# A routed LayerNorm moved ahead of a rotation, the first loads split over two queues, and one wait shortened in a gated cross-attention and expert kernel

## The chip, the cores and the metric

The kernel runs on one core of a Trainium2 chip. The metric is the device time of one execution in microseconds (us). The program is written engine by engine: TensorE (PE, with its weight loads as PEld), VectorE (DVE), ScalarE (ACT), GpSimd (POOL) and the DMA queue of SyncE (SP) each have an instruction stream of their own, and all order between them is by semaphores that the program counts by hand. An engine executes its stream in order, so an instruction that waits holds up everything behind it on that engine.

## The reference

The input x holds 16 batches of 112 rows of 512 values. Each batch has a context of 375 rows of 128 values.

```python
x = x + tanh(g_xattn[0]) * xattn(layernorm(x), ctx, ...)   # 16 heads, latent scores, rotation of q and of the context
x = x + tanh(g_ffn[0])   * ffn(layernorm(x), ...)          # 64 experts, 8 chosen for each row, and one shared expert
```

The attention projects the normalised x for each head (`Wq`), turns the result into a 384-wide latent (`w_kc_q`), rotates it with tables of cosines and sines, folds it with `W_qr` and `W_kr` into 128 values that meet the rotated context, and takes a softmax. The feed-forward part sends each row of the second normalised x to the 8 experts with the highest logits.

## The kernel before

The 16 batches are worked in four groups of four (`GB`). A group has two stages.

**The head stage** is a loop over h from 0 to 17 in `tensor`, `vector`, `scalar`, `gpsimd` and `sync` alike. In its turn h, TensorE projects head h (`project`, 12 products of 448 columns), makes the latent of head h-1 (`latent`, 9 products, lines 822 to 824 in both cases), and takes head h-2 to the context space (`to_context`, line 926). DVE makes the low half of each projection (line 1245), multiplies the latent with the cosine and sine tables in seven operations a head (`latent`, lines 1270 and 1274), and makes the low half of what goes to the context space (line 1280). GpSimd adds the cosine and sine parts in three operations a head (line 1940). ACT makes the high halves.

**The score stage** is a loop over 56 tiles of scores (`RT` = 14 for each batch) with softmax, transposes (line 955) and the product with the context. The output projection of the group follows (`out_head`), and DVE adds it to x (line 1342).

**The routing** of finished batches is woven into the head stage of the next group. `slots(g, i)` gives each step of batch i of group g a slot, `between(g, slot)` lists the steps of a slot, and turn h of the head loop carries slots 2h and 2h+1. For the first batch of a group the steps are statistics in slot 0 (DVE line 1323, then GpSimd lines 1904 and 1906 with the power of -0.5), "norm" in slot 2 (DVE line 1399), "turn" in slot 3 (TensorE's four transposes, line 1028, and ACT's copy, line 1741), "router" in slot 4 (line 1040), "choose" in slot 5. On DVE, slot 2 stands behind the seven operations of head 0's rotation; slots 0 and 1 stand ahead of the projection of head 1. On TensorE and ACT nothing stands between slot 2 and slot 3 of turn 1. SP stores the normalised rows and the new x (`finish` in `sync`, lines 666 and 667) `STORE_LAG` = 4 slots after their "norm", so for the first batch at the head of turn 3, behind its reloads of weights.

**The end of the last group.** Batches 13 to 15 have nothing to hide their routing behind. When the last tiles of scores are under way, TensorE begins the output projection of batch 15 (`out_head` with p = `NG`); it goes into bank 7, which also holds the ranks of batch 12. Ahead of its first head TensorE waits until all of batch 12's routing steps are counted:

```python
if p == NG and h == 0:
    pe.wait_ge(s_exp, RT * B)
    pe.wait_ge(s_route, NR * (B - GB + 1))
```

DVE reads the ranks in the first operation of `put_in_place` (line 1376); three more operations make the places and one adds to the count (line 1384). GpSimd's scatters of batches 13, 14 and 15 (line 1962) come after that, and the experts after them.

**The start.** SP issues the identity matrix and the constant -0.5 (lines 538 and 539, both on semaphore `s_first`), then the four batches of x (line 544), then weights. DVE waits for `s_first`, writes five small pads, takes statistics of the four batches, and normalises batches 0 and 1 into two buffers (`xn1`). Batches 2 and 3 are normalised in the same two buffers once TensorE has transposed the batch before (`s_xt`), between the low halves (line 1234) of batches 0 and 1. ACT copies the first weights (line 1667) ahead of the high halves of x (line 1646). TensorE's first projection needs all four batches.

Of the kernel before, what the change touches and what calls it, by code (L numbers as in the profile page):

```python
# [11 lines left out]
ALU = mybir.AluOpType  # L12
# [4 lines left out]
B, S, C = 16, 112, 512  # L17
# [5 lines left out]
P = 128  # L23
# [6 lines left out]
GB = 4  # L30
# [30 lines left out]
def shape_constants():  # L61

    sq, cq = rope_tables(S, Q)
    sk, ck = rope_tables(L, D)

    sr = np.concatenate([-sq[:, :QH], sq[:, QH:]], axis=1)
    skn = np.concatenate([-sk[:, :D // 2], sk[:, D // 2:]], axis=1)
    cq, sr = cq[:, PERM], sr[:, PERM]
    sr[:, 2 * QW:] = np.concatenate([sr[:, -QW // 2:], sr[:, 2 * QW:-QW // 2]], axis=1)
    qt = lambda a: np.ascontiguousarray(a.T.reshape(QC, QW, S).transpose(1, 0, 2))  # L70
    lt = lambda a: np.ascontiguousarray(a.reshape(LJ, LP, D).transpose(1, 0, 2))
    tri = np.triu(np.ones((S, S), np.float32), 1)
    return {
        "c_cos_q": qt(cq), "c_sin_q": qt(sr), "c_cos_k": lt(ck), "c_sin_k": lt(skn),
        "c_ident": np.eye(P, dtype=np.float32),
        "c_before": tri,
        "c_ones": np.ones((S, P), np.float32),
        "c_expert": np.tile(np.arange(E, dtype=np.float32), (S, 1)),
        "c_minus_half": np.full((P, 1), -0.5, np.float32),


        "c_spare": np.ascontiguousarray(np.arange(P * (3 * NY + 1), dtype=np.float32).reshape(3 * NY + 1, P).T),
        "c_own_row": SPARE + np.arange(S, dtype=np.float32)[:, None] * KY + np.arange(TOP, dtype=np.float32),
        "c_expert_entries": np.tile(np.arange(E, dtype=np.float32) * SPAN, (S, 1)),
        "c_lower_first": np.tile(-np.arange(E, dtype=np.float32) / E, (E, 1)),
        "c_lower_own": -np.arange(E, dtype=np.float32)[:, None] / E,
        "c_number": np.tile(np.arange(E, dtype=np.float32)[:, None], (1, P)),
        "c_caps": np.asarray(CAPS, np.float32)[None, :],
    }
# [46 lines left out]
def slots(g, i):  # L136

    at = START[LEFT[g]][i]
    whole = {"turn": at + 3, "router": at + 4, "choose": at + 5, "rank": at + 7, "place": at + 8}
    if g:  # L140
        whole.update({f"scatter {k}": at + 9 + (k * 7 // 8 if i == 2 else k) for k in range(TOP)})
    return {"stats": max(0, at - 2), "norm": max(2, at), **(whole if i < GB - LEFT[g] else {})}

# [98 lines left out]
def x_bank(b):  # L242
    return 4 + b if b < GB else 7
# [39 lines left out]
def build(nc, a, out):  # L283
    with ExitStack() as ctx:
# [3 lines left out]
        def sem(name):  # L288
            return ctx.enter_context(nc.semaphore(name))
# [108 lines left out]
        q_t = [sb(f"q_t{p}", [D, GB, H, S], F32R) for p in "hl"]  # L398

        def q_rows(part, b, at, width):  # L400
            return q_t[part][:, b % GB, :, :].rearrange("d h s -> d (h s)")[:, at:at + width]
# [44 lines left out]

        s_first, s_const, s_late, s_zero = sem("s_first"), sem("s_const"), sem("s_late"), sem("s_zero")
        s_const_k = sem("s_const_k")
# [88 lines left out]
        def sync(sp):  # L537
            sp.dma_start(ident[:], a["c_ident"]).then_inc(s_first, 16)
            sp.dma_start(minus_half[:], a["c_minus_half"]).then_inc(s_first, 16)

            def load_x(b):
# [126 lines left out]

            for b in range(GB):
                load_x(b)  # L670
            load_wq(0)
# [147 lines left out]
        def tensor(pe):  # L819
# [6 lines left out]
            def turn_x(b):  # L826
# [7 lines left out]
                for j in range(CJ):  # L834
                    m = pe.transpose(bank[x_bank(b)][:, j * S:(j + 1) * S], xn1[b % 2][:, j * P:(j + 1) * P],
                                     ident[0:S, 0:S])
# [140 lines left out]
            def out_head(p, h, part):  # L977
# [13 lines left out]
                if p == NG and h == 0:  # L991
                    pe.wait_ge(s_exp, RT * B)
                    pe.wait_ge(s_route, NR * (B - GB + 1))
                if part != "first":
# [61 lines left out]

            pe.wait_ge(s_first, 32)
            for b in range(GB):
# [155 lines left out]
        def vector(dve):  # L1214
# [9 lines left out]
            def norm_x(b):  # L1224
                st = ln_stats[min(b, GB)]
                if b >= 2:
                    dve.wait_ge(s_xt, b - 1)
                dve.wait_ge(s_rs1, 2 * (b + 1))
                dve.tensor_scalar(xn1[b % 2][:], x_sb[b % NX][:], st[:, 6:7], st[:, 0:1], ALU.subtract, ALU.mult)\
                   .then_inc(s_nm1, 1)  # L1230
# [187 lines left out]

            dve.wait_ge(s_first, 32)
            for part in (*kv_t[0], *kv_t[1]):  # L1420
                dve.tensor_scalar(part[:, L:L + 1], ident[:, 0:1], 0.0, None, ALU.mult).then_inc(s_pad, 1)
            dve.memset(count[:], 0.0).then_inc(s_pad, 1)
            for b in range(GB):
                stats_x(b)
            norm_x(0)
            norm_x(1)
            for b in range(GB):
                turn_x(b)
                if b + 2 < GB:
                    norm_x(b + 2)  # L1430

# [209 lines left out]
        def scalar(act):  # L1641
# [94 lines left out]
            def finish(step, b):  # L1736
# [6 lines left out]
                if step == "choose":  # L1743
                    act.wait_ge(s_route, NR * b + R_SHIFT)
                    act.activation(raised[:], top[:], ACT.Exp, bias=small[:, 0:1], accum_out=small[:, 1:2])\
                       .then_inc(s_weigh, 1)

            split_wq(0)
            for b in range(GB):
# [151 lines left out]
        def gpsimd(pool):  # L1901
# [62 lines left out]

            pool.wait_ge(s_first, 32)
            for b in range(GB):
# [123 lines left out]
```

## Time and profile before

| | |
|---|---|
| median of 3 runs | 1543.54 us (1543.45 to 1543.58) |
| the profiled execution, own time | 1545.0 us |
| its span in the profile | 1543.1 us |
| PE busy | 1419.2 us, 92% |
| DVE busy | 1147.3 us, 74% |
| POOL busy | 783.3 us, 51% |
| ACT busy | 672.1 us, 44% |

The span is the time between the first and the last instruction that the profile shows; 1.9 us of the execution lie around it. Busy times of different engines overlap. A matmul's duration is modelled and reaches over the start of the next one, so the step from start to start is its cost in a chain. The rows quoted further down give the start in us, the duration in us, the engine, the line, the operation with output and input, and in brackets how long the engine had been idle before and what ended the idleness.

### The profile page before, as it was taken

To read this page: it belongs to the slowest core of one execution; us is meant where nothing else is said; L and a number is where in the kernel's file an instruction comes from. 1 tells how busy PE (TensorE), PEld (TensorE's weight loads), DVE (VectorE), ACT (ScalarE), POOL (GpSimd) and SP (SyncE) were. 2 spreads that over 40 slices of the span, in tenths; PEclk is the share of its full clock that TensorE was granted. 3 is DMA by queue.
4 is the path that set the end of the run, shared out by engine and by line. 5 is a ranking of instruction groups with operands and counts; after the bars stand their busy time and mean duration, and the time that the engine had idled before them with its cause. 6 is when DMAs were issued, how large, how long until landed. Compare 5 with 4: busy or idle time off the path is not lost.

```text
span 1543.1 us, 25067 instructions
## 1 busy us (share of the span) xinstructions
PE 1419.2 (92%) x7674; PEld 1165.1 (76%) x7674; DVE 1147.3 (74%) x2601; ACT 672.1 (44%) x1558; POOL 783.3 (51%) x858
## 2 busy tenths in 40 slices
PE   6999899899999989999989999986399999989985
PEld 5767787777788777778877778864388999979742
DVE  5777783298987269989528988544488999979587
ACT  3332673011476011177301137431277777867521
POOL 4555673145775458877345786325344344334322
PEclk9999999999999999999999999998599999999998
DMA  7898896355697757830365763295899999999698
GB/s 238 298 313 314 274 286 193 112 167 188 215 307 219 265 162 246 253 122 8 104 217 191 243 216 113 86 341 180 239 331 327 332 357 366 373 339 338 206 429 344
DMA packets 164359, 380.10 MB, mean 246 GB/s; under 512 B 20200, under 2 KB 55682, under 8 KB 162434
## 3 DMA queue, kind: packets, MB, share of 16 engines
q1 hardware_dynamic: 136182, 286.33, 55.5%
q0 software_dynamic: 20608, 62.28, 11.8%
q10 hardware_dynamic: 7436, 29.88, 6.0%
q8 instruction: 64, 1.05, 0.3%
q14 instruction: 69, 0.57, 0.1%
HBM read 238.82 MB, written 139.59 MB: 245 GB/s over the span
## 4 chain that ended last, share of the span: by engine, by line
PE 71%; DVE 10%; DMA 9%; issue 5%; POOL 2%; ACT 2%; SPq 1%; POOLq 0%; another core or an unknown queue 0%; DVEq 0%; ACTq 0%
PE bank L822 18%; PE bank L824 17%; PE bank L823 17%; PE bank L926 8%; PE bank L955 4%; DMA p_in<-parts 3%; PE bank L1124 2%; DMA parts<-y_sb,to_row 1%; DMA w_ex<-in_w_ex 1%; PE bank L914 1%; PE bank L904 1%; DMA out<-p_sum 1%; DVE prob_t0l L1309 1%; POOL slot_rows L1962 1%; ACT prob L1705 1%
## 5 line engine op out<-in xcount | busy, mean ns | idle before, releaser
L1940 POOL TENSOR_TENSOR q_rope<-q_rope,q_sin 128x448 f32<-128x448 f32 x192 | 215.7, 1153 | 147.4 <-DVE q_sin L1274 146.8
L2020 POOL DMA_INDIRECT parts<-y_sb,to_row x140 | 138.3, 988 | 221.0 <-ACT y_sb L1846 191.4
L1946 POOL TENSOR_TENSOR prob<-prob,row_inv 128x375 f32<-128x375 f32 x219 | 176.8, 814 | 88.7 <-DVE row_inv L1296 86.5
L1962 POOL DMA_INDIRECT slot_rows<-rows,pos_i x112 | 109.7, 980 | 104.2 <-DVE count L1384 76.8
L1274 DVE TENSOR_TENSOR q_sin<-bank,sin_q 128x448 f32<-128x448 f32 (+1 forms) x256 | 158.5, 619 | 4.0
L926 PE MATMUL bank<-q_rope,m_w 128*128 128x448 f32 x384 | 155.7, 541 | 2.8 <-issue 1.8
L1288 DVE TENSOR_REDUCE row_max<-bank 128x1 f32<-128x375 f32 x224 | 118.9, 535 | 36.8 <-PE bank L824 36.4
L1705 ACT ACTIVATE prob<-bank,row_max 128x375 f32<-128x375 f32 x224 | 128.3, 573 | 9.1 <-DVE row_max L1288 9.1
L1846 ACT ACTIVATE y_sb<-bank,own 96x512 f32<-96x512 f32 (+4 forms) x140 | 90.9, 687 | 68.6 <-PE bank L824 62.0
L955 PE MATMUL bank<-ident,prob 128*125 128x128 f32 x672 | 113.6, 279 | 7.1 <-DVE prob_t0l L1309 3.6
L1270 DVE TENSOR_TENSOR q_rope<-bank,cos_q 128x448 f32<-128x448 f32 x192 | 118.3, 616 | 0.0
L955 PEld LDWEIGHTS bank<-ident,prob 128*125 128x125 f32 x672 | 103.6, 189 | 15.9 <-POOL prob L1946 13.1
L926 PEld LDWEIGHTS bank<-q_rope,m_w 128*128 128x128 f32 x384 | 71.5, 189 | 53.4 <-issue 50.3
L1688 ACT ACTIVATE q_th<-bank 128x448 fp32r<-128x448 f32 x64 | 34.9, 545 | 170.6 <-PE bank L926 156.4
L1681 ACT ACTIVATE q_hk0h<-bank 128x448 fp32r<-128x448 f32 x32 | 17.5, 546 | 160.4 <-PE bank L824 160.4
L1720 ACT ACTIVATE prob_t0h<-bank 125x384 fp32r<-125x384 f32 x128 | 63.0, 492 | 46.0 <-PE bank L955 46.0
L1124 PE MATMUL bank<-ident,x_g 96*128 96x96 f32 (+4 forms) x560 | 64.5, 261 | 20.0 <-DMA x_g<-slot_rows 20.0
L1124 PEld LDWEIGHTS bank<-ident,x_g 96*128 96x128 f32 (+4 forms) x560 | 59.5, 144 | 29.6 <-DMA x_g<-slot_rows 20.5
L822 PE MATMUL bank<-xg_t0h,w_gu_s0h 128*128 128x224 f32 (+5 forms) x256 | 75.9, 297 | 4.9 <-DVE e_half L1529 4.9
L1342 DVE SCALAR_TENSOR_TENSOR x_sb<-bank,tanh_g,x_sb 112x512 f32<-112x512 f32 x16 | 11.3, 746 | 88.5 <-PE bank L824 88.5
L822 PE MATMUL bank<-xg_t1h,w_gu_s1h 128*128 128x224 f32 (+5 forms) x256 | 73.9, 289 | 0.7 <-DVE e_half L1529 0.6
L823 PE MATMUL bank<-xg_t0l,w_gu_s0h 128*128 128x224 f32 (+5 forms) x256 | 73.2, 286 | 0.0
(364 smaller groups left out, 4399.1 us busy)
## 6 DMA issues: line engine op xcount, KB each, us to landing
w_ex<-in_w_ex SPq DMA_DIRECT2D x64, 768.0 KB
slot_rows<-blank SPq DMA_DIRECT2D x64, 612.0 KB
p_in<-parts SPq DMA_DIRECT2D x14, 2048.0 KB, 16.9
m_w<-m_dram SPq DMA_DIRECT2D x48, 192.0 KB
x_g<-slot_rows ACTq DMA_DIRECT2D x16, 476.0 KB
wq_s0h<-wq_dram SPq DMA_DIRECT2D x24, 256.0 KB
wq_s0l<-wq_dram SPq DMA_DIRECT2D x24, 256.0 KB
wq_s1h<-wq_dram SPq DMA_DIRECT2D x24, 256.0 KB
```

The lines of the kernel that those rows point to most:

```text
L822: pe.matmul(out_ap, wh, mh, start=first, stop=False)
L823: pe.matmul(out_ap, wh, ml, start=False, stop=False)
L824: return pe.matmul(out_ap, wl, mh, start=False, stop=last)
L926: m = pe.matmul(bank[5][:, 0:GT], m_w[n % NW][:, c, :], q_rope[h % 2][:, c, :], start=(c == 0), stop=(c == QC - 1))
L955: m = pe.transpose(bank[bk][0:LP, j * P:(j + 1) * P], prob[n % NP][:, j * LP:(j + 1) * LP], ident[:])
L1124: m = pe.transpose(bank[n % 3][:, j * size:(j + 1) * size], x_g[x % NXE][0:size, t, j * P:(j + 1) * P], ident[0:size, 0:size])
L1274: dve.tensor_tensor(q_sin[to:to + size, other, :].rearrange("p (b s) -> p b s", b=GB), src[at:at + size], table, ALU.mult).then_inc(s_rope, 1)
L1705: act.activation(prob[i][:], bank[score_bank(n)][:, 0:L], ACT.Exp, bias=row_max[:, i:i + 1], accum_out=row_sum[:, i:i + 1]).then_inc(s_exp, 1)
L1940: pool.tensor_tensor(o[:, c, :], o[:, c, :], q_sin[:, c, :], ALU.add).then_inc(s_radd, 1)
L1946: pool.tensor_tensor(prob[i][:], prob[i][:], row_inv[:, i:i + 1].to_broadcast([P, L]), ALU.mult)\
L1962: pool.indirect_dma_start(slot_rows, bass.IndirectOffsetOnAxis(ap=pos_i[i][:, k:k + 1], axis=0), rows[i][:], None).then_inc(s_slots[i], 16)
L2020: pool.indirect_dma_start(parts, bass.IndirectOffsetOnAxis(ap=to_row[x % NROW][0:size, t:t + 1], axis=0), y_sb[x % NY][t][0:size, :], None)\
```

## The change

For the first batch of each group's routing, "norm" goes to slot 1 and "turn" to slot 2. The loads of x alternate between SP (batches 0 and 2) and ACT (batches 1 and 3), and the identity follows them. The constant -0.5 is written by GpSimd instead of loaded. The normalised batches 2 and 3 of the first group go into two of the `rows` buffers, which are free at the start, so that all four are normalised in a row, ahead of the low halves and the pads. The wait ahead of batch 15's output projection asks for batch 12's ranks to be read (`R_RANKED`), not for its count.

```diff
-        "c_minus_half": np.full((P, 1), -0.5, np.float32),
...
-    whole = {"turn": at + 3, "router": at + 4, "choose": at + 5, "rank": at + 7, "place": at + 8}
+    whole = {"turn": at + (3 if i else 2), "router": at + 4, "choose": at + 5, "rank": at + 7, "place": at + 8}
...
-    return {"stats": max(0, at - 2), "norm": max(2, at), **(whole if i < GB - LEFT[g] else {})}
+    return {"stats": max(0, at - 2), "norm": at if i else 1, **(whole if i < GB - LEFT[g] else {})}
...
+        def xn1_of(b):
+            return rows[b - 2][:, 0:C] if 2 <= b < GB else xn1[b % 2][:]
...
         def sync(sp):
-            sp.dma_start(ident[:], a["c_ident"]).then_inc(s_first, 16)
-            sp.dma_start(minus_half[:], a["c_minus_half"]).then_inc(s_first, 16)
-
...
-            for b in range(GB):
-                load_x(b)
+            load_x(0)
+            load_x(2)
+            sp.dma_start(ident[:], a["c_ident"]).then_inc(s_first, 16)
             load_wq(0)
...
                 if p == NG and h == 0:
                     pe.wait_ge(s_exp, RT * B)
-                    pe.wait_ge(s_route, NR * (B - GB + 1))
+                    pe.wait_ge(s_route, NR * (B - GB) + R_RANKED)
...
-            pe.wait_ge(s_first, 32)
+            pe.wait_ge(s_first, 16)
...
             def norm_x(b):
                 st = ln_stats[min(b, GB)]
-                if b >= 2:
+                if b >= GB:
                     dve.wait_ge(s_xt, b - 1)
...
-            dve.wait_ge(s_first, 32)
+            for b in range(GB):
+                stats_x(b)
+            for b in range(GB):
+                norm_x(b)
+            for b in range(GB):
+                turn_x(b)
+            dve.wait_ge(s_first, 16)
             for part in (*kv_t[0], *kv_t[1]):
                 dve.tensor_scalar(part[:, L:L + 1], ident[:, 0:1], 0.0, None, ALU.mult).then_inc(s_pad, 1)
             dve.memset(count[:], 0.0).then_inc(s_pad, 1)
-            for b in range(GB):
-                stats_x(b)
-            norm_x(0)
-            norm_x(1)
-            for b in range(GB):
-                turn_x(b)
-                if b + 2 < GB:
-                    norm_x(b + 2)
...
+            for b in (1, 3):
+                act.dma_start(x_sb[b][:], a["x"][b * S:(b + 1) * S, :]).then_inc(s_x[b], 16)
             split_wq(0)
...
-            pool.wait_ge(s_first, 32)
+            pool.memset(minus_half[:], -0.5).then_inc(s_half, 1)
+            pool.wait_ge(s_half, 1)
             for b in range(GB):
                 spread(ln_stats[b], s_bn1, s_rs1, b)
```

## Rows read from the trace of the kernel before

**Rows 1.** The page: the chain that ended last, shares of the span by engine.

```profile
PE 71%; DVE 10%; DMA 9%; issue 5%; POOL 2%; ACT 2%; SPq 1%; POOLq 0%; another core or an unknown queue 0%; DVEq 0%; ACTq 0%
```

**Rows 2.** PE's waits: instruction, releaser: us in total, times, longest.

```profile
PE bank L1028 <- DVE rows L1399: 19.3, 4, 7.9
...
PE bank L1028 <- DVE early_rows L1399: 4.2, 1, 4.2
```

**Rows 3.** Timeline of PE at the start of the second group's head stage.

```profile
292.62 0.36 PE L822 MATMUL bank<-xn_th,wq_s0h 128*128 128x448 f32 x1
...
297.49 0.37 PE L822 MATMUL bank<-q_hk0h,wcq_s0h 128*128 128x448 f32 x1
...
303.65 1.01 PE L1028 MATMUL bank<-ident,early_rows 112*128 112x112 f32 x4 [4.17 <-DVE early_rows L1399]
...
309.95 0.91 PE L1040 MATMUL bank<-token_w,xn_t 128*112 128x64 f32 x8
```

**Rows 4.** Timeline of PE: the same two steps in the third and fourth groups.

```profile
554.35 1.01 PE L1028 MATMUL bank<-ident,rows 112*128 112x112 f32 x4 [4.17 <-DVE rows L1399]
561.47 0.91 PE L1040 MATMUL bank<-token_w,xn_t 128*112 128x64 f32 x8
...
806.42 1.01 PE L1028 MATMUL bank<-ident,rows 112*128 112x112 f32 x4 [4.17 <-DVE rows L1399]
813.78 0.91 PE L1040 MATMUL bank<-token_w,xn_t 128*112 128x64 f32 x8
```

**Rows 5.** Stretches: start:end, length, busy of PE, PEld, DVE, ACT, POOL, PEclk, DMA, GB/s.

```profile
304.00:307.00 3.00, 3.00 (x11) 2.74 (x10) 0.00 (x0) 0.54 (x1) 0.59 (x1) 0.50 0.03 10
...
330.00:340.00 10.00, 10.00 (x40) 7.35 (x39) 9.84 (x20) 1.29 (x3) 4.49 (x6) 1.00 0.48 156
```

**Rows 6.** Timeline of PE: the same transposes at full clock.

```profile
502.79 0.55 PE L1028 MATMUL bank<-ident,rows 112*128 112x112 f32 x4
```

**Rows 7.** Timelines of POOL and DVE around the second group's first norm.

```profile
297.67 0.57 POOL L1906 TENSOR_TENSOR ln_stats<-ln_stats,minus_half 112x1 f32<-112x1 f32 x1
301.09 3.50 POOL L1940 TENSOR_TENSOR q_rope<-q_rope,q_sin 128x448 f32<-128x448 f32 x3 [2.86 <-DVE q_sin L1274]
...
298.26 0.62 DVE L1245 TENSOR_TENSOR q_hk1l<-bank,q_hk1h 128x448 fp32r<-128x448 f32 x1 [0.99 <-ACT q_hk1h L1681]
...
302.89 0.71 DVE L1399 TENSOR_SCALAR early_rows<-x_sb,ln_stats 112x512 f32<-112x512 f32 x1
```

**Rows 8.** Timelines around the wait ahead of batch 15's output projection (DVE, PE, POOL).

```profile
1041.49 0.20 DVE L1376 TENSOR_TENSOR rank_sb<-bank,expert_entries 112x64 f32<-112x64 f32 x1
...
1043.98 0.55 DVE L1309 TENSOR_TENSOR prob_t0l<-bank,prob_t0h 125x384 fp32r<-125x384 f32 x1
...
1044.32 0.74 PE L822 MATMUL bank<-v_w0h,q_th 128*112 128x512 f32 x1 [3.23 <-DVE count L1384]
...
1064.53 0.94 POOL L1962 DMA_INDIRECT slot_rows<-rows,pos_i  x1 [10.51 <-DVE count L1384]
```

**Rows 9.** Stretch from that matmul on; columns as in rows 5.

```profile
1044.30:1048.20 3.90, 3.88 (x13) 3.18 (x14) 0.23 (x1) 0.33 (x1) 2.99 (x4) 0.56 0.48 91
```

**Rows 10.** Timelines of the first 16 us: SP's issues of x, then DVE, ACT, PE.

```profile
1.65 1.83 SPq L544 DMA_DIRECT2D x_sb<-in_x  x4
...
8.20 0.69 DVE L1220 BATCH_NORM_STATS2 ln_stats<-x_sb 112x6 f32<-112x512 f32 x1
...
0.74 1.28 ACT L1667 ACT_TABLE_LOAD   x1 [0.74 <-PEq L2081]
9.27 0.64 ACT L1667 ACTIVATE wq_s0h<-wq 128x512 fp32r<-128x512 f32 x1 [7.25 <-DMA wq<-in_w_q]
...
9.69 1.73 PE L835 MATMUL bank<-ident,xn 112*128 112x112 f32 x8 [9.69 <-DVE xn L1229]
12.41 2.00 PE L835 MATMUL bank<-ident,xn 112*128 112x112 f32 x8 [1.00 <-DVE xn L1229]
15.79 0.71 PE L822 MATMUL bank<-xn_th,wq_s0h 128*128 128x448 f32 x1 [1.38 <-DVE xn_tl L1234]
```

More of the change, by code:

```diff
@@ L445, in build @@
         base_in = early_base + [x for _, x in late_tiles]
-        s_first, s_const, s_late, s_zero = sem("s_first"), sem("s_const"), sem("s_late"), sem("s_zero")
+        s_half, s_first, s_const, s_late, s_zero = sem("s_half"), sem("s_first"), sem("s_const"), sem("s_late"), sem("s_zero")
         s_const_k = sem("s_const_k")
@@ L834, in turn_x @@
                 for j in range(CJ):
-                    m = pe.transpose(bank[x_bank(b)][:, j * S:(j + 1) * S], xn1[b % 2][:, j * P:(j + 1) * P],
+                    m = pe.transpose(bank[x_bank(b)][:, j * S:(j + 1) * S], xn1_of(b)[:, j * P:(j + 1) * P],
                                      ident[0:S, 0:S])
@@ L1225, in norm_x @@
                 st = ln_stats[min(b, GB)]
-                if b >= 2:
+                if b >= GB:
                     dve.wait_ge(s_xt, b - 1)
                 dve.wait_ge(s_rs1, 2 * (b + 1))
-                dve.tensor_scalar(xn1[b % 2][:], x_sb[b % NX][:], st[:, 6:7], st[:, 0:1], ALU.subtract, ALU.mult)\
+                dve.tensor_scalar(xn1_of(b), x_sb[b % NX][:], st[:, 6:7], st[:, 0:1], ALU.subtract, ALU.mult)\
                    .then_inc(s_nm1, 1)
```

## The prediction

> **What bounds the kernel now.** I read the chain that ended last, then PE's waits, then the timelines at the places where PE waited. TensorE holds 71% of the chain [rows 1], so time is gained only where PE stands idle or runs slowly. PE's waits name the transposes of the routed rows among the largest items, with VectorE's norm as the releaser: four times in `rows` and once in `early_rows` [rows 2]. The timeline puts three of them at the same place of the second, third and fourth group, each after exactly 4.17 us of idle time [rows 3, 4]. There PE has finished head 0's latent and comes to "turn", while the norm is still behind head 0's rotation on DVE: DVE begins it at 302.89, although GpSimd had its scale ready at 297.67 + 0.57 = 298.24 [rows 7]. After each idle stretch PE works at half clock, 0.50 for the 3 us from 304 to 307 [rows 5]. The largest remaining `rows` wait, 7.9 us, belongs to batch 15 at the end, which the change does not touch.
>
> **Norm and turn.** "Norm" passes from slot 2 to slot 1: on DVE it moves ahead of head 1's low half and head 0's seven rotation operations. "Turn" passes from slot 3 to 2, with nothing between them on PE and ACT, so their orders stay. What matters is whether the rows are ready when PE arrives. In the first head stage 24 products run from 292.62 to 297.49, 0.203 us a step, and nine more bring PE to the transposes at 299.32 [rows 3]. The norm can start at 298.24 and takes 0.71 [rows 7], so it ends at 298.95, 0.37 ahead. I take the wait as gone.
>
> The price of a group goes from idle start to the router. Now: 4.17 idle and 309.95 - 303.65 = 6.30 of work [rows 3], 7.12 and 7.36 in the next two groups [rows 4]. The work is four transposes, 12 products and 9 products. At full clock the transposes take 0.55 [rows 6] and 21 products 21 x 0.203 = 4.26, in all 4.81. The groups give back 4.17 + 1.49, 4.17 + 2.31 and 4.17 + 2.55, together **18.9 us**. If the clock fell all the same, 12.5 would be left; nothing that PE would wait for here makes it fall. The upper end is 19.6, since the last transpose's 0.2 overlaps the next product.
>
> What becomes late next: DVE's low half of head 1 starts at 298.95 instead of 298.26, and so the rotation of head 0 and GpSimd's three adds come 0.7 later, the adds at 301.8 to 305.3 instead of 301.09 to 304.59 [rows 7]. PE needs the first of them at 299.32 + 4.81 + the router's 0.91 = 305.0, and the last only after two thirds of that step. So that costs nothing, but the cover shrinks to some tenths of a us; without it the 0.7 would be paid three times, 2.1. From then on DVE has little air: it is busy 9.84 of 10 us in a later stretch of the stage, with PE busy throughout [rows 5]. It starts at most 0.7 later in relation to PE than before, and each head's output goes through double buffers, so I put this at nothing, with the 2.1 in the range. On GpSimd, the scatters of slots 0 and 1 stand ahead of the adds in the third and fourth group, as now; they had time while DVE worked, and their order does not change. SP stores the rows and the new x one place earlier, ahead of the next reload of projection weights and behind one reload of `m_w`; two issues of 0.46 (a quarter of 1.83, [rows 10]) delay that reload by 0.9, and it is needed a whole head later. Nothing, and at worst 0.9 for each group.
>
> **Batch 15's projection.** PE stands idle for 3.23 us until 1044.32 for batch 12's count, while the ranks had been read at 1041.49 + 0.20 = 1041.69 [rows 8]. With the shorter wait PE goes on some 0.1 later, 2.5 us sooner. What follows is the next-to-last tile, then the last tile, which cannot start before DVE's split that begins at 1043.98 and ends at 1044.53 [rows 8]; so a short idle returns there. Against this stands the clock: 3.90 us at 0.56 after the old wait [rows 9] cost some 3.90 x 0.44 = 1.7, of which part comes back if it stays up. Lower end 1.5 (the split is waited for and the clock falls again), upper end 3.5, taken **2.5**. It reaches the end: GpSimd's scatters of batch 13 had been idle for 10.51 us until 1064.53 [rows 8], and they and all behind them follow from this PE work.
>
> **The start.** The last batch of x is issued last of four on SP, at 1.65 + 1.83 = 3.48, its statistics begin at 8.20, and PE's first product at 15.79 [rows 10]. That is 7.59 from statistics to product. With four buffers the transposes of four batches follow each other: the first starts 9.69 - 8.20 = 1.49 after the last statistics, two batches take 1.73, the other two 2.00, then a high and a low half of some 0.55 and 0.62 and a few tenths of handing over, about 6.5. That is 1.05 without any earlier transfer. ACT's two issues can be out by 1.7 if they go ahead of the table load, or by 2.94 if they stand behind its end at 2.02 [rows 10]: 1.8 or 0.5 earlier than 3.48. The weights' copy on ACT at 9.27 [rows 10] stands ahead of the high halves; its load is issued 1.4 earlier, and if it landed at 9.27 as now, the high halves would still be done before the transposes allowed more. Pads on DVE, GpSimd's memset in place of a load and the later identity are all ready before anything needs them, which costs nothing; if the five pads stood in the way, 0.4. Together 1.05 + 0.5 to 1.05 + 1.8, with 4.5 as the far end if the half-speed stretch after the first product moved too; taken **2.5**.
>
> The long time from issue to statistics, 8.20 - 3.48 = 4.72 for one batch, looks like transfers that share what moves them. The Trainium skill ("DMA: Bandwidth & Descriptors", "Issuing engines are not separate DMA queues") says that loads started by different engines run on the same 16 DMA engines, and that issuing from several saves only sequencer time. By that the second queue brings no bandwidth, and the start's term would be the first rival's below; no row before shows two queues loading x at once, so the trace leaves it open.
>
> **Sum.** 18.9 + 2.5 + 2.5 = 23.9 us. Against the profiled execution, 1545.0 - 23.9 = 1521.1. That execution lies 1.5 above the median of 1543.54, so the median should come to 1519.6; I say 1519.5.
>
> **The rivals.**
>
> Start without a gain from transfers: x lands when it does now, because the DMA engines are the limit. Then the start gives 1.05, and the median is 1543.5 - 18.9 - 2.5 - 1.05 = 1521.0. For it speaks that PE's start hangs on 4.7 us of transfer; against it, that the first issue is 0.9 earlier. Chance 0.2.
>
> Only the idle time returns: the clock falls at other places instead, or the 0.37 us margin of the norm is not there and PE still stops briefly. Then three times 4.17, 1.5 and 1.05 are left, 15.1, which gives 1528.4. For it speaks the small margin and the shrunken cover on GpSimd; against it that all PE waits of this stage disappear with the norm. Chance 0.14.
>
> Slower: DVE executes in order, and in slot 1 it waits for GpSimd's power with head 1's low half and the whole rotation behind it, which before had nothing to wait for. If GpSimd is late by d, PE loses d less about 1 us in each group, and the half clock besides. The point from which this is slower than now is d = 23.9 / 3 + 1 = 9 us a group; with d = 12 the time would be 1543.5 + 9 = 1552.5. It needs GpSimd to be held up by scatters ahead of the statistics. In the group shown it had answered by 298.24 [rows 7], so there is no such d. Chance 0.02.
>
> The change does not do what it says, because the turn on PE is held by something else that came at the same time as the norm: no gain but the start and the end, 1538.5, chance 0.02. No gain at all, chance 0.02.
>
> **How the numbers follow.** The forecast as summed has 0.6. The range takes the start's far end, the clock's return and the rest of a late 0.7 us, and reaches most of the way to the second rival: 1515.5 to 1527.0. A measurement of this kernel tells about 0.2%, 3.1 us, from no change. Forecast and first two rivals are all well over that and so is most of the fourth: faster 0.95; "no gain" and a part of the fourth make same 0.03; slower 0.02.
>
> **What would show it.** In the new profile, the three 4.17 us gaps ahead of the routed transposes should be gone, the granted clock should stay at 1.00 there, and transposes to router should take 4.8. DVE's norm should stand ahead of head 1's low half. The wait for the count should be a wait for the ranks of under 1 us, with a new short wait ahead of the last tile's transposes. The first product should start near 13.3. I would be wrong if a new wait for GpSimd's adds or for reloaded weights stood in the second to fourth head, or if PE lost elsewhere what it gained at the turns.

## The result, and the profile after

The changed kernel takes 1522.31 us (median of 4 runs, 1521.71 to 1524.49), the kernel before 1543.56 in the same comparison. The ratio is 0.9864, with a 95% interval of 0.9847 to 0.9881: 18 to 24 us faster. The forecast was 1519.5 with a range of 1515.5 to 1527.0. The profiled execution of after took 1521.71 us of its own time, with a span of 1519.9; that of before had a span of 1543.1, so the two profiles differ by 23.2.

Below, "lead" is how much earlier than in the profile of before an instruction of TensorE starts. Line numbers of the new kernel are 2 to 4 lower: the routed transposes are L1026, the norm L1397, the router L1038, the products L820 to L822.

First the busy times of the page of after.

```profile
PE 1407.8 (93%) x7674; PEld 1156.0 (76%) x7674; DVE 1148.8 (76%) x2601; ACT 672.3 (44%) x1558; POOL 783.2 (52%) x859
```

PE is busy 11.4 us less than the 1419.2 of before with the same instructions. The work behind the three turns, which no longer runs at the lower clock, makes 6.7 of that by the rows below. PE still holds 70% of the chain that ended last [rows 1]. The rest of the gain is idle time.

PE's waits (instruction, releaser: us in total, times, longest) answer to [rows 2].

```profile
PE bank L1026 <- DVE rows L1397: 10.9, 2, 7.8
...
PE bank L953 <- POOL prob L1944: 3.7, 1, 3.7
...
PE bank L820 <- DMA wq_s1l<-wq_dram: 1.2, 1, 1.2
...
PE bank L820 <- DMA wq_s0l<-wq_dram: 1.0, 1, 1.0
```

The wait for `early_rows` is gone and that for `rows` has two cases in place of four. The 7.8 us case is batch 15's at the end, as before. Two short waits for reloaded weights stand out, 1.2 and 1.0; in the profile of before they were 0.4 and 0.2.

The timeline of PE at the three places of [rows 3, 4], in the second, third and fourth group:

```profile
298.66 0.55 PE L1026 MATMUL bank<-ident,early_rows 112*128 112x112 f32 x4
...
303.38 0.91 PE L1038 MATMUL bank<-token_w,xn_t 128*112 128x64 f32 x8
...
543.43 0.55 PE L1026 MATMUL bank<-ident,rows 112*128 112x112 f32 x4
...
548.10 0.91 PE L1038 MATMUL bank<-token_w,xn_t 128*112 128x64 f32 x8
...
789.39 0.55 PE L1026 MATMUL bank<-ident,rows 112*128 112x112 f32 x4
...
794.05 0.91 PE L1038 MATMUL bank<-token_w,xn_t 128*112 128x64 f32 x8
```

No idle time stands in brackets, and the transposes take 0.55 in place of 1.01. From transposes to router it is 4.72, 4.67 and 4.66 us, where it was 6.30, 7.12 and 7.36. A stretch of that work (start:end, length, busy of PE, PEld, DVE, ACT, POOL, granted clock, DMA, GB/s) answers to the 0.50 of [rows 5]:

```profile
299.00:302.00 3.00, 3.00 (x18) 2.74 (x16) 2.97 (x6) 0.81 (x2) 1.10 (x1) 1.00 0.58 152
```

On DVE and GpSimd the same place now reads as follows (compare [rows 7]).

```profile
297.01 0.57 POOL L1904 TENSOR_TENSOR ln_stats<-ln_stats,minus_half 112x1 f32<-112x1 f32 x1
300.90 3.36 POOL L1938 TENSOR_TENSOR q_rope<-q_rope,q_sin 128x448 f32<-128x448 f32 x3 [3.32 <-DVE q_sin L1272]
...
297.62 0.55 DVE L1397 TENSOR_SCALAR early_rows<-x_sb,ln_stats 112x512 f32<-112x512 f32 x1 [1.00 <-POOL ln_stats L1904]
298.08 0.62 DVE L1243 TENSOR_TENSOR q_hk1l<-bank,q_hk1h 128x448 fp32r<-128x448 f32 x1
```

The norm stands ahead of head 1's low half and ends at 298.17, some 0.5 us ahead of PE's 298.66. The bracket on the norm is the one new wait in this stage, and it costs nothing: before, DVE stood the same time there, 0.99 us, for ACT's high half [rows 7].

The start, in the timelines of SP's and ACT's queues, DVE and PE, answers to [rows 10]:

```profile
0.73 0.87 SPq L541 DMA_DIRECT2D x_sb<-in_x  x2
0.73 0.91 ACTq L1745 DMA_DIRECT2D x_sb<-in_x  x2
...
6.52 0.66 DVE L1218 BATCH_NORM_STATS2 ln_stats<-x_sb 112x6 f32<-112x512 f32 x1
...
7.97 1.73 PE L833 MATMUL bank<-ident,xn 112*128 112x112 f32 x8 [7.97 <-DVE xn L1227]
8.20 2.48 DVE L1227 TENSOR_SCALAR rows<-x_sb,ln_stats 112x512 f32<-112x512 f32 x2
10.28 1.75 PE L833 MATMUL bank<-ident,rows 112*128 112x112 f32 x8 [0.58 <-DVE rows L1227]
13.42 0.71 PE L820 MATMUL bank<-xn_th,wq_s0h 128*128 128x448 f32 x1 [1.39 <-DVE xn_tl L1232]
```

The first product starts at 13.42, 2.37 earlier. The last issue of x ends at 1.64 in place of 3.48, and its statistics begin at 6.52 in place of 8.20.

At the end (compare [rows 8]):

```profile
1022.10 0.20 DVE L1374 TENSOR_TENSOR rank_sb<-bank,expert_entries 112x64 f32<-112x64 f32 x1
...
1022.56 0.46 PE L820 MATMUL bank<-v_w0h,q_th 128*112 128x512 f32 x1 [0.86 <-DVE rank_sb L1374]
...
1025.28 0.56 PE L953 MATMUL bank<-ident,prob 128*125 128x128 f32 x3 [0.78 <-DVE prob_t0l L1307]
...
1038.22 0.94 POOL L1960 DMA_INDIRECT slot_rows<-rows,pos_i  x1 [3.60 <-DVE count L1382]
```

The wait is for the ranks, 0.86 long, and a new one of 0.78 stands ahead of the last tile's transposes.

Following the lead through the kernel tells where the time came from and where some went. It is 2.4 at the first product, but only 0.7 at 172 us, in group 0's score stage. It rises by 5.9, 6.8 and 7.0 at the three turns, stands at 19.4 before batch 15's projection and at 26.3 after it, and is 23.2 at the end.

The loss at 172 us has this view, of SP's queue, GpSimd, PE and two stretches, and no row in the prediction:

```profile
157.55 0.35 SPq L643 DMA_DIRECT2D kv_raw<-in_ctx  x1
...
163.72 0.99 POOL L1921 TENSOR_TENSOR kv_full<-kv_raw,cos_k 125x384 f32<-125x384 f32 x1 [3.91 <-DMA kv_raw<-in_ctx]
...
165.53 1.00 PE L953 MATMUL bank<-ident,prob 128*125 128x128 f32 x3 [3.69 <-POOL prob L1944]
...
162.50:167.50 5.00, 1.97 (x8) 1.97 (x9) 1.39 (x4) 0.93 (x3) 3.78 (x6) 0.72 1.05 376
167.50:172.50 5.00, 5.00 (x19) 4.18 (x19) 1.63 (x6) 2.21 (x7) 4.09 (x5) 0.60 0.97 309
```

The same place in the profile of before:

```profile
160.05 0.36 SPq L646 DMA_DIRECT2D kv_raw<-in_ctx  x1
...
165.61 0.99 POOL L1923 TENSOR_TENSOR kv_full<-kv_raw,cos_k 125x384 f32<-125x384 f32 x1 [3.29 <-DMA kv_raw<-in_ctx]
...
167.42 1.00 PE L955 MATMUL bank<-ident,prob 128*125 128x128 f32 x3 [3.10 <-POOL prob L1946]
```

GpSimd waits 3.91 us for the context of the second batch, with its scaling of probabilities behind it, and PE waits 3.69 for these; before, the waits were 3.29 and 3.10. The load is issued 2.50 earlier than before, as much as PE is ahead there, so this transfer moved along with the rest; in this execution it took 0.6 longer. The larger part, 1.2 us, goes behind the wait: over the 5 us from the end of the wait the granted clock is 0.50, and over the same 5 us in the profile of before it is 0.69. The earlier start is neither needed for this loss nor enough for it. The kernel with the shorter wait only, whose start is that of before, takes 1.1 us more than before behind the same wait, at a clock of 0.50. The changed kernel's second profile takes 0.1 more at the wait and 0.1 more behind it, at a clock of 0.67. How long the lower clock lasts behind this wait comes and goes with the execution.

### The profile page after: what moved, and what is told of

It is laid out like the page before. It is cut to its first block, busy times and chain, and to the rows that moved or that the text cites. A ratio compares the mean times of both kernels' runs of the same rounds, so it can differ in the third digit from the quotient of the medians.

```text
span 1519.9 us, 25065 instructions
## 1 busy us (share of the span) xinstructions
PE 1407.8 (93%) x7674; PEld 1156.0 (76%) x7674; DVE 1148.8 (76%) x2601; ACT 672.3 (44%) x1558; POOL 783.2 (52%) x859
## 3 DMA queue, kind: packets, MB, share of 16 engines
q0 software_dynamic: 20608, 62.28, 12.1%
q8 instruction: 64, 1.05, 0.3%
## 4 chain that ended last, share of the span: by engine, by line
PE 70%; DMA 12%; DVE 9%; issue 4%; POOL 3%; ACT 2%; SPq 0%; POOLq 0%; ACTq 0%; DVEq 0%
PE bank L820 18%; PE bank L822 17%; PE bank L821 17%; PE bank L924 9%; PE bank L953 4%; DMA p_in<-parts 3%; DMA w_ex<-in_w_ex 3%; DMA parts<-y_sb,to_row 3%; PE bank L1122 2%; POOL slot_rows L1960 1%; PE bank L912 1%; PE bank L1038 1%; PE bank L902 1%; DVE prob_t0l L1307 1%; DMA out<-p_sum 1%
## 5 line engine op out<-in xcount | busy, mean ns | idle before, releaser
L820 PE MATMUL bank<-xg_t0h,w_gu_s0h 128*128 128x224 f32 (+5 forms) x256 | 74.8, 292 | 4.2 <-DVE e_half L1525 4.2
L820 PE MATMUL bank<-xg_t1h,w_gu_s1h 128*128 128x224 f32 (+5 forms) x256 | 73.8, 288 | 5.1 <-DVE e_half L1525 5.0
```

The lines of the kernel that those rows point to most:

```text
L820: pe.matmul(out_ap, wh, mh, start=first, stop=False)
```

## The experiments

Eleven kernels ran, in three sets. Kernels of a set share a chip and its runs of the kernel before. Its median was 1543.68 in the first set, 1547.01 in the second and 1547.79 in the third. Single runs of one kernel lie several us apart, so I read ratios with their intervals and, for what is smaller, places in the traces. A ratio is an estimate from all the runs and not the quotient of the two medians.

### First set: each part of the change alone

**Slots only.** The kernel before with

```diff
-    whole = {"turn": at + 3, "router": at + 4, "choose": at + 5, "rank": at + 7, "place": at + 8}
+    whole = {"turn": at + (3 if i else 2), "router": at + 4, "choose": at + 5, "rank": at + 7, "place": at + 8}
...
-    return {"stats": max(0, at - 2), "norm": max(2, at), **(whole if i < GB - LEFT[g] else {})}
+    return {"stats": max(0, at - 2), "norm": at if i else 1, **(whole if i < GB - LEFT[g] else {})}
```

> Only norm and turn one slot earlier. Theory A (the turn waits and their slow stretches are the main gain, parts add up): all three 4.17 us gaps gone, 19 to 20 us less than before. Rival B (what is gained at the turns is partly lost again to late weight loads, because the stores of the first batch now stand ahead of a reload): one or two new DMA waits of about 1 us ahead of a projection, directly behind the moved stores (fourth head of a group), and only 17 to 18 us less.

Measured: 1524.14 (5 runs), ratio 0.9868 (0.9845 to 0.9890), 19.5 us by the medians. This part alone is most of the change. The one wait for a reloaded weight that stands out is 0.6 us long. Of its two edits only the one of "norm" does anything: with "turn" put back to `at + 3` in the changed kernel, the instructions stand in the same order on all five engines, since slots 2 and 3 belong to the same turn of the loop. That is read from the order of the programs and needed no run.

**Start only.** The kernel before with the loads over two queues and the four buffers, and with what goes along with them: the identity behind x, the -0.5 written by GpSimd, the pads behind the norms. The diff shows the main lines.

```diff
-            for b in range(GB):
-                load_x(b)
+            load_x(0)
+            load_x(2)
+            sp.dma_start(ident[:], a["c_ident"]).then_inc(s_first, 16)
...
+            for b in (1, 3):
+                act.dma_start(x_sb[b][:], a["x"][b * S:(b + 1) * S, :]).then_inc(s_x[b], 16)
...
-                dve.tensor_scalar(xn1[b % 2][:], x_sb[b % NX][:], st[:, 6:7], st[:, 0:1], ALU.subtract, ALU.mult)\
+                dve.tensor_scalar(xn1_of(b), x_sb[b % NX][:], st[:, 6:7], st[:, 0:1], ALU.subtract, ALU.mult)\
```

> Only the start. Theory A (everything behind the start shifts with it): first product near 13.4 us instead of 15.8, time 2.4 us less. Rival B (the context of batch 1 lands when the DMA lets it, so the score stage of the first group eats the lead): first product near 13.4 too, but the lead of 2.4 falls to 0.6 to 1.9 at 165 us, with a longer PE wait for GpSimd's normalised tile (3.7 us instead of 3.1), time 0.5 to 2 us less.

**Loads only.** The same without the four buffers (norms and turns interleaved over two buffers, as before).

> The loads over two queues, the later identity, GpSimd's -0.5 and the pads behind, but two buffers as before. Theory A (both halves of the start's change count: earlier landing 1.3, four buffers 1.05): first product near 14.5 us. Rival B (the transfers land when the DMA engines allow, so only issue time is saved): first product 15.3 or later. Time between 0.3 and 1.5 us less than before.

Measured: start 1542.39, ratio 0.9979 (0.9960 to 0.9998); loads alone 1543.90, ratio 0.9987 (0.9972 to 1.0001). The first interval ends just short of 1 and the second includes it, so only the traces tell the parts. PE's first product, in the kernel with loads only and in that with both:

```profile
7.75 1.73 PE L832 MATMUL bank<-ident,xn 112*128 112x112 f32 x8 [7.75 <-DVE xn L1226]
...
13.86 0.71 PE L819 MATMUL bank<-xn_th,wq_s0h 128*128 128x448 f32 x1 [1.39 <-DVE xn_tl L1231]
```

```profile
7.94 1.73 PE L835 MATMUL bank<-ident,xn 112*128 112x112 f32 x8 [7.94 <-DVE xn L1229]
...
13.39 0.71 PE L822 MATMUL bank<-xn_th,wq_s0h 128*128 128x448 f32 x1 [1.39 <-DVE xn_tl L1234]
```

The loads bring the first product from 15.79 to 13.86, 1.93. From the first transposes to it the two-buffer kernel needs 6.11 us (6.10 before), the four-buffer one 5.45: the buffers give 0.65, not 1.05. These are single profiles: in the other kernels with the new start the first product comes at 13.23 to 13.47 six times, and at 14.37 and 14.94 where x landed later; in those with the old one at 15.15, 15.71 and 15.79. At 172 us the lead of the kernel with both has fallen from 2.4 to 1.2. That is the number of the expectation's rival, but not its mechanism: PE's wait for the context is 3.0 us, not 3.7, and the time goes behind it, at the lower clock.

**The shorter wait only.**

```diff
-                    pe.wait_ge(s_route, NR * (B - GB + 1))
+                    pe.wait_ge(s_route, NR * (B - GB) + R_RANKED)
```

> Only the wait ahead of batch 15's output projection. Theory A (as predicted: the idle time and a part of the clock): 2.5 us less than before, at most 3.5. Rival B (the short gap also keeps the clock at 1.00 through the heads behind it, and takes the later wait for the turned rows along): 6 to 7 us less, GpSimd's scatter of batch 13 starts 6 to 7 us earlier.

Measured: 1540.74, ratio 0.9981 (0.9967 to 0.9996), 0.6 to 5.1 us. The lead grows by 6.9 us at this place in the profile of after, and by 6.2 here, against 2.5 forecast. The three kernels of this set that keep the long wait show why that comparison misleads. From the transposes ahead of the wait to those of the routed rows behind it (1040.53 to 1052.58 in the profile of before) they take 12.47, 12.50 and 12.54 us, before 12.05; with the shorter wait it is 9.78 here and 9.11 after. That is 2.3 to 3.4, about 3. The lower figure is the one at which the clock fell again: behind the short wait it is 0.57 for 4.0 us here, and 1.00 in the profile of after. The rest of the lead, some 3.5 us, belongs to the profile of before alone; the kernel with the start only gains as much there with the long wait. In its timeline PE goes on at 1056.22 after a wait for `xn_t`; the kernel with the start only, same code at this place, has none:

```profile
1052.58 0.55 PE L1028 MATMUL bank<-ident,rows 112*128 112x112 f32 x4
...
1055.53 0.54 ACT L1741 ACTIVATE xn_t<-bank 128x448 f32<-128x448 f32 x1 [1.06 <-remote]
...
1056.22 0.97 PE L1040 MATMUL bank<-token_w,xn_t 128*112 128x64 f32 x8 [2.40 <-ACT xn_t L1741]
```

```profile
1052.46 0.55 PE L1028 MATMUL bank<-ident,rows 112*128 112x112 f32 x4
...
1053.04 0.55 ACT L1739 ACTIVATE xn_t<-bank 128x448 f32<-128x448 f32 x1
...
1053.73 0.97 PE L1040 MATMUL bank<-token_w,xn_t 128*112 128x64 f32 x8
```

From one to the other it is 3.64 us in the first and 1.27 in the second. What held ACT, the trace does not name.

### Second set: variants of the changed kernel

> The changed kernel once more, as the measure for its variants and for the spread. Theory: the comparison of the profile of before with those of three kernels that keep its routed batch as it is shows that the profile of before holds two stretches of its own: a 2.4 us wait for xn_t at 1056 and half clock from 1058 to 1061, which the others lack (they gain 2.7 to 3.0 us between 1031 and 1060 against it), and an experts stage of 433.6 us from the second wait for x_g to the end, where the others take 435.5 to 436.7. If so, this execution again has neither the xn_t wait nor an experts stage under 435, and its median is 1519 to 1524. Rival: the expert stage of the changed kernel is longer because of the change; then a stage of 436 here as well, but kernels with the slots as before would not have shown it.

Measured: 1521.80, ratio 0.9853 (0.9825 to 0.9880). The expectation held for the time and for the experts stage: 436.2 us, counted from the second wait for gathered rows, where the profile of before has 433.6 and the twelve others of this study 433.4 once and 434.4 to 436.7 eleven times. So the 2.5 us that the change seemed to hand back there need no cause in it: the three other kernels with the old slots show 435.4 to 436.7 against this one execution of before. It failed for the late `xn_t`: transposes to router took 2.36 us, where the first profile of this same kernel has 1.27. So the delay is not made by the change. The four kernels of the first set all have 1.27 or 1.28, the seven of the other two sets all 2.29 to 3.35, the profile of before 3.64; it goes with the set of runs, and its cause is open.

**The second batch's context earlier.** In SP's program:

```diff
+                    if g == 0 and h == 12:
+                        load_context(1)
...
-                        if t == 0 and g == 0:
-                            load_context(1)
```

> The changed kernel with the load of the second batch's context issued in the thirteenth head of group 0 instead of behind the last weight store. Theory: group 0's score stage hands back part of the earlier start because GpSimd stands 3.9 us for this load, and PE 3.7 us for GpSimd's prob, after which it works at 0.60 to 0.72 for 10 us. Then this wait is gone, PE's lead at the end of the stage grows by 3.7 to 6.5 us, and the median is 4 to 6 us under that of the changed kernel. Rival: another wait stands right behind it (the copy of x ahead of the score stage, ACT or DVE), and 1 to 2 us come out. Second rival: the load is not what is late (the wait named is an inference), nothing changes.

Measured: 1518.58 (5 runs, 1514.84 to 1520.64), ratio 0.9811 (0.9789 to 0.9832). The changed kernel has 0.9853 in the same set. The timeline and stretches of this kernel:

```profile
125.08 0.35 SPq L643 DMA_DIRECT2D kv_raw<-in_ctx  x1
...
161.27 1.01 POOL L1921 TENSOR_TENSOR kv_full<-kv_raw,cos_k 125x384 f32<-125x384 f32 x1
...
163.69 0.56 PE L953 MATMUL bank<-ident,prob 128*125 128x128 f32 x3
...
160.00:165.00 5.00, 4.27 (x26) 3.55 (x26) 5.00 (x13) 4.30 (x14) 4.07 (x6) 1.00 0.91 294
165.00:170.00 5.00, 4.93 (x29) 4.33 (x30) 3.95 (x13) 3.97 (x12) 4.75 (x7) 1.00 1.01 329
```

Both waits are gone and the clock stays at 1.00. Behind this place PE stands 4.2 us ahead of the profile of after and 2.8 ahead of the changed kernel's second profile, although its first product was 1.5 later in this execution (14.94, x landed later). So the place gave back 5.7 against the one, whose clock was low for long, and 4.3 against the other. In the median it is 3.2, a little under the 4 to 6 that I expected.

**The two stores back at their old place.**

```diff
+                    if g and h == 3:
+                        finish("norm", (g - 1) * GB)
...
+                        if (step, b) != ("norm", (g - 1) * GB):
                             finish(step, b)
```

> The changed kernel with SP's two stores of the first routed batch back at their old place in the fourth head. Theory, as predicted: the place of the two issues costs nothing, the time is that of the changed kernel within 1 us, and the two waits of PE for reloaded projection weights (1.0 and 1.2 us in groups 2 and 3) are still there, since they stand some nine heads behind the stores and come from PE being ahead of the other transfers. Rival: the moved stores make these waits; then both are gone and 2 us come back.

Measured: 1521.66 (4 runs), ratio 0.9836 (0.9813 to 0.9859), against 1521.80 in the same set. The place of the stores is worth nothing that I can measure. On the waits the expectation was wrong: only one of 0.3 us is left here. But they come and go with the execution of one and the same kernel: 1.2 and 1.0 in the profile of after, a single one of 1.1 in its second profile, and none over 0.6 in the kernel with the slots only, which has the stores moved as well. What makes them is open.

**GpSimd late, first try.** Four extra multiplications of 125x384 ahead of GpSimd's scale for the first routed batch of each group.

```diff
+                if step == "stats" and b in (0, 4, 8):
+                    pool.wait_ge(s_krope, 6 * (b + GB + 1))
+                    for k in range(4):
+                        pool.tensor_tensor(kv_tmp[:], cos_k[:], cos_k[:], ALU.mult).then_inc(s_half, 1)
+                        pool.wait_ge(s_half, b // GB * 4 + k + 2)
                 if step == "stats":
                     spread(ln_stats[b % GB], s_bn2, s_rs2, b)
```

> The changed kernel with GpSimd held back by four extra multiplications of 125x384 (about 0.99 us each) ahead of its scale for the first routed batch, in each of the three groups, so that VectorE's norm in slot 1 starts about 4 us late. By the prediction's slower rival PE loses d less a margin: about 3.6 us of idle and the half clock behind it, 1.5 to 2.5 us, in each group: 15 to 18 us over the changed kernel, 1537 to 1541. If DVE's queue behind the norm (head 1's low half, the rotation) makes PE wait a second time, it is more, up to the time of before or over it. Rival: the margin is larger than 0.4 us since DVE reaches the norm later than GpSimd answers; then 12 us or less.

Measured: 1522.17, ratio 0.9843 (0.9820 to 0.9866), no loss. That is under the rival's 12 us, but not for its reason. The timeline of GpSimd shows that I had put the load where it delays nothing:

```profile
244.37 3.55 POOL L1956 TENSOR_TENSOR kv_tmp<-cos_k 125x384 f32<-125x384 f32 x4
...
295.23 0.22 POOL L1902 TENSOR_SCALAR ln_stats<-ln_stats 112x1 f32<-112x1 f32 x1 [47.32 <-DVE ln_stats L1323]
```

The extra work stands in the queue ahead of the wait for DVE's statistics, and GpSimd is idle for some 50 us there. That still says something: work ahead of that wait, which was the condition of my slower rival, would have to be some 50 us long in this group before it mattered. In the next two groups there is less room. There a row of scatters, the very work that the rival named, stands ahead of the wait, and the idle time behind it is 12.1 us in both; in the changed kernel's third group:

```profile
541.47 0.23 POOL L1902 TENSOR_SCALAR ln_stats<-ln_stats 112x1 f32<-112x1 f32 x1 [12.09 <-DVE ln_stats L1323]
```

### Third set: GpSimd late behind the statistics

The same multiplications between the wait for the statistics and the scale (`late` is true for the routed batches 0, 4 and 8), four of them and twelve.

```diff
                 pool.wait_ge(s_bn, 2 * (b + 1))
+                if late:
+                    pool.wait_ge(s_krope, 6 * (b + GB + 1))
+                    for k in range(4):
+                        pool.tensor_tensor(kv_tmp[:], cos_k[:], cos_k[:], ALU.mult).then_inc(s_half, 1)
+                        pool.wait_ge(s_half, b // GB * 4 + k + 2)
                 pool.tensor_scalar(st[:, 0:1], st[:, 7:8], EPS, None, ALU.add).then_inc(s_rs, 1)
```

> As d4_late, but GpSimd's four extra multiplications stand behind its wait for VectorE's statistics instead of ahead of it, where GpSimd had been idle for 47 us and hid them. Now the norm in slot 1 must start about 4 us late (301.6 in place of 297.6). By the slower rival of the prediction PE loses d less its margin, about 3.4 us of idle a group, and the half clock behind it, about 1.5 to 2.5: 15 to 18 us over the changed kernel, a median of 1536 to 1540. If VectorE's queue behind the norm adds a second wait of PE, for head 1's low half or GpSimd's adds, it is more. If PE recovers the loss in the same head stage, less.

> The same with twelve extra multiplications, d = 12 us a group. By the prediction's formula (loss d - 1 a group) 1522 + 33 = 1555, slower than before; with the half clock behind each wait up to 1562. The prediction's point from which the change is slower than before was d = 9. Rival: VectorE's queue makes PE wait a second time in each group; then over 1565. Rival: the loss saturates since other work of PE can be caught up; then under 1545.

Measured: 1536.46, ratio 0.9931 (0.9910 to 0.9952), and 1561.01, ratio 1.0096 (1.0070 to 1.0122), both inside the expectation. Timelines of GpSimd, DVE and PE in the second group, four multiplications and then twelve:

```profile
295.08 3.55 POOL L1905 TENSOR_TENSOR kv_tmp<-cos_k 125x384 f32<-125x384 f32 x4 [50.64 <-DVE ln_stats L1323]
...
299.62 0.55 DVE L1397 TENSOR_SCALAR early_rows<-x_sb,ln_stats 112x512 f32<-112x512 f32 x1 [4.62 <-POOL ln_stats L1909]
...
300.23 0.60 PE L1026 MATMUL bank<-ident,early_rows 112*128 112x112 f32 x4 [3.02 <-DVE early_rows L1397]
...
306.50 0.91 PE L1038 MATMUL bank<-token_w,xn_t 128*112 128x64 f32 x8
```

```profile
294.93 10.79 POOL L1905 TENSOR_TENSOR kv_tmp<-cos_k 125x384 f32<-125x384 f32 x12 [50.74 <-DVE ln_stats L1323]
...
307.32 1.01 PE L1026 MATMUL bank<-ident,early_rows 112*128 112x112 f32 x4 [10.27 <-DVE early_rows L1397]
...
314.06 0.91 PE L1038 MATMUL bank<-token_w,xn_t 128*112 128x64 f32 x8
```

A delay of 3.55 gives PE 3.02 us of idle time, one of 10.79 gives 10.27: the margin is 0.53 and 0.52. Behind it the 4.72 us to the router become 6.27 and 6.74. That is 4.6 and 12.3 us a group, three times 13.7 and 36.9; the medians rose by 14.4 and 39.0 over the 1522.05 midway between the changed kernel's two. PE waits for nothing else here: head 1's low half follows the norm at once, and to_context stands behind the router without a wait.

**Early context and stores behind together.** Both diffs of the second set.

> The version with the second batch's context loaded in group 0's thirteenth head, together with SP's two stores at their old place. Theory: the places of the two stores are worth nothing, the waits for reloaded projection weights (0 to 1.2 us, present or absent in executions of one and the same order of stores) are not made by them; median 1517 to 1520, as with the early context alone (1518.6). Rival: the stores cost up to 2 us together with the earlier PE; then 1516 to 1517.

Measured: 1517.62 (5 runs, 1516.43 to 1520.13), ratio 0.9814 (0.9794 to 0.9834), as with the early context alone, 0.9811. It is the context that beats both kernels; the stores' place again adds nothing.

## Why the prediction was right, point by point

**Norm and turn: right, mechanism and size.** In place, the groups gave 4.17 + 1.58, 4.17 + 2.45 and 4.17 + 2.70, together 19.2 against 18.9. By the starts, which the lead follows, it is 19.7, just over my upper end of 19.6: a bracket counts from the modelled end of the matmul before, which overlaps the next by 0.16. The margin of the norm, 0.37 by the rows of before, is 0.5 in three ways of reading it. GpSimd's first add began at 300.90, behind the norm, the low half and four operations of the rotation, and PE found it done when it came to it, so "nothing" for DVE's lateness held.

**Batch 15's projection: right, sized low.** 2.3 to 3.4 against 2.5 (range 1.5 to 3.5). The short wait ahead of the last tile came as said, 0.78, and at the full clock in the changed kernel; with the shorter wait only, the clock fell, as my lower end had it. The 6.9 that a comparison of the two profiles shows here is not this term.

**The start: right sum from wrong parts.** 2.37 at the first product against 2.5. The loads gave 1.93, above the 0.5 to 1.8 that I allowed, and the buffers 0.65 of time from transposes to product, where I had 1.05: DVE's two norms into `rows` took 2.48 us together, where two such norms took 0.97 before. The last load of x took 4.8 us from the start of its issue to its landing, before 5.1; over all profiles it is 4.5 to 6.3 in the ten with two queues and 4.5 to 5.1 in the three with one. So nothing shows the second queue to move x faster. What came earlier is the issues, by 1.84, and half of that, 0.92, is not the second queue's: the identity and the constant no longer stand ahead of x on SP. x is then complete at 6.0 in place of 8.2. DVE no longer waits for it but works through the four batches without a stop from 4.10, and so begins the last statistics only at 6.52. By the Trainium skill ("DMA: Bandwidth & Descriptors", "Issuing engines are not separate DMA queues") issue time is all that a second issuing engine saves, and the traces do not speak against it. The step of mine that failed is the one from this rule to my first rival, 1521.0: I read "no bandwidth" as "no gain", although 1.83 us of issues stood on the path.

**What I left out, and what stays open.** The terms sum to some 24.6 in place of my 23.9, yet the medians differ by 21.3. In the second set they differ by 25.2, and a saving of 24.6, a ratio of 0.9841, lies just outside the first interval and inside the second (0.9825 to 0.9880). So the runs do not show that a term is missing. Nothing in the prediction asks what lies between the start and the first turn. There the profile of after loses 1.7 us and its second profile 0.3, at a wait for the context that the profile of before had already shown, 3.10 on PE; most of the 1.7 is the clock behind the wait, which a kernel with the old start lost as well. The waits for reloaded weights are 1.6 more in the profile of after and 0.5 more in the second one. Whether the 3 us between this sum and the first comparison are more than the scatter of the runs stays open.

**The chances.** Of the rivals, "only idle returns" (1528.4) is out, since the clock stayed at 1.00. The slower one has its mechanism, shown in the third set, but not its condition: GpSimd is idle for 50 us ahead of the statistics in the second group, and for 12 in the third and fourth, behind its scatters. Its price for the idle time was half a us too low in each group (d less 0.5, not less 1), and its point was wrong: I set it at 9 us a group, leaving the half clock out. Between the two delays measured, 24.6 us more for 7.24 of delay or 3.4 for one, the change is used up at 5.6 to 6.9 us: 3.55 + (21.5 - 14.4) / 3.4 = 5.6 by the 1543.56 of before, 6.9 by the 1547.79 of the third set.

## What to carry to other kernels

A short operation on which the next engine hangs belongs ahead of the long sequence that merely shares its queue; here one entry in a table of slots gave 19.5 us, where the whole change gave 21.3, and it was safe because its own input was ready 0.5 us before it was missed. Look for waits on a transfer also where the change touches nothing: the one for the second batch's context stood in the profile of before, and moving its issue 33 us ahead was worth 3.2 us in the median, not less than the start. And before a difference between two profiles is explained, look at the same place in a third one that shares the code there; it took that to see that the 6.9 us at batch 15's projection, the 2.5 us in the experts stage and the 1.2 us behind the context's wait were not the change's.

## What the runs showed of the hardware

PE's stop costs more than its idle time, but not in proportion to it. At the three turns, the work to the router took longer than at full clock by 1.6 us behind 3.02 to 3.13 us of idle (three readings), by 1.4 to 2.9 behind 4.17 (twelve, in the four kernels with the old slots), and by 1.5 to 2.5 behind some 10.3 (three). The spread between executions is larger than what the length of the stop adds.

DVE's norm of 112x512 takes 0.54 when it stands alone, and two of them took 2.48 us at 8.20: the first 2.03, the second 0.54. GpSimd worked on its own statistics and on the low half of the weights meanwhile. All nine profiles with four buffers show it, with 2.48 or 2.49. Whether the buffer or GpSimd's work is the cause was not tried.

One kernel's executions spread over more than its first three runs let one think: the kernel before had 1543.45 to 1543.58 there and 1536.58 to 1553.69 in 27 runs of the first set.
